# A two-layer perceiver block on one core: who sends the shift row, where the exponents stand and how the column maxima are taken in the second layer's context attention

## The reference, cut to what matters

```python
q = query @ Wq.T + bq
k = key @ Wk.T + bk
v = value @ Wv.T + bv
scores = jnp.einsum('bhtd,bhsd->bhts', q, k) * scale
attn = jax.nn.softmax(scores, axis=-1)
ctx = jnp.einsum('bhts,bhsd->bhtd', attn, v)
return ctx.transpose(0, 2, 1, 3).reshape(B, T, D_MODEL) @ Wo.T + bo
```

## Time and profile before

| What | Value |
|---|---|
| median of 3 runs | 3909.35 us (3906.99 to 3917.72) |
| time of the profiled execution | 3923.12 us, of which the span is 3921.2 us |
| PE busy over the span | 3746.8 us (96%) |
| DVE, ACT, POOL busy | 2212.4, 1525.4 and 1012.3 us |
| the stage that is changed | from about 2427 to 3640 us of the span |

### The profile page before, as it was taken

How to read it: one execution, slowest core, us unless ns; L and a number is a source line. 1 busy time by engine, 2 the same in 40 slices (tenths; PEclk the granted TensorE clock), 3 DMA queues, 4 the chain that set the end, 5 groups by cost and what they waited for, 6 DMA issues and landing times. The chain is left out here.

```text
span 3921.2 us, 73601 instructions
## 1 busy us (share of the span) xinstructions
PE 3746.8 (96%) x29918; PEld 2714.0 (69%) x29918; DVE 2212.4 (56%) x4864; ACT 1525.4 (39%) x3725; POOL 1012.3 (26%) x857
## 2 busy tenths in 40 slices
PE   8999999999999999999999999999999999999897
PEld 4777777777777777867756556666666666667785
DVE  4555555555555545535555413676676766766557
ACT  3233222232323323224433222555555555565444
POOL 2020201011010202002221021354554554553222
PEclk9999999999999999999999999999999999999999
DMA  4112222212121212120040574212212212101100
GB/s 151 61 59 65 65 65 65 65 55 72 48 65 44 80 42 85 54 71 23 24 134 28 169 263 127 63 20 66 65 24 66 63 26 64 52 20 31 37 2 23
DMA packets 159837, 254.81 MB, mean 65 GB/s; under 512 B 28112, under 2 KB 66640, under 8 KB 157712
## 3 DMA queue, kind: packets, MB, share of 16 engines
q1 hardware_dynamic: 121872, 188.15, 15.2%
q0 software_dynamic: 13104, 47.98, 3.7%
q10 hardware_dynamic: 24528, 13.96, 1.7%
HBM read 216.97 MB, written 33.10 MB: 64 GB/s over the span
## 5 line engine op out<-in xcount | busy, mean ns | idle before, releaser
L581 PE MATMUL swishmax_attended<-swishmax_weights_t,swishmax_context 128*128 128x128 f32 x4096 | 520.1, 275 | 3.4 <-DVE swishmax_values_t L505 3.4
L1561 POOL TENSOR_TENSOR context_partial<-context_partial,context_weights_t 128x512 f32<-128x512 f32 x300 | 382.4, 1275 | 466.4 <-ACT context_weights_t L1589 449.9
L435 ACT ACTIVATE swishmax_xes<-swishmax_score,swishmax_neg_max 128x512 f32<-128x512 f32 x256 | 177.1, 694 | 806.9 <-DVE swishmax_neg_max L470 806.9
L581 PEld LDWEIGHTS swishmax_attended<-swishmax_weights_t,swishmax_context 128*128 128x128 f32 x4096 | 487.9, 192 | 3.8 <-issue 3.8
L1770 PE MATMUL context_bank<-ahead_stream,ahead_staged 128*128 128x512 f32 x1024 | 485.3, 617 | 3.1 <-PEq L1138 1.7
L595 PE MATMUL swishmax_bank<-ahead_stream,ahead_w 128*128 128x512 f32 x1024 | 464.2, 596 | 7.4 <-DMA ahead_stream<-in_context_t_dram 7.4
L581 PE MATMUL swishmax_attended<-swishmax_weights_t,swishmax_sides 128*128 128x128 f32 x3072 | 384.9, 275 | 0.0
L581 PEld LDWEIGHTS swishmax_attended<-swishmax_weights_t,swishmax_sides 128*128 128x128 f32 x3072 | 363.6, 192 | 0.0
L1770 PEld LDWEIGHTS context_bank<-ahead_stream,ahead_staged 128*128 128x128 f32 x1024 | 189.0, 195 | 213.4 <-issue 199.0
L1779 PEld LDWEIGHTS context_bank<-ahead_w,ahead_stream 128*128 128x128 f32 x2304 | 276.9, 192 | 80.6 <-issue 55.3
L1670 DVE TENSOR_TENSOR context_weights_t<-context_weights_t,context_spread 128x512 f32<-128x512 f32 x512 | 314.7, 679 | 30.1 <-ACT context_spread L1585 25.9
(11 more groups left out here) (379 smaller groups left out, 5787.3 us busy)
## 6 DMA issues: line engine op xcount, KB each, us to landing
ahead_stream<-in_context_t_dram SPq DMA_DIRECT2D x78, 1024.0 KB, 6.1
swishmax_context<-in_context_dram POOLq DMA_DIRECT2D x32, 1024.0 KB, 5.7
swishmax_down<-_L_xattn_value_down_dram SPq DMA_DIRECT2D x64, 256.0 KB, 4.3
swishmax_up<-in_L_xattn_value_up_dram SPq DMA_DIRECT2D x32, 512.0 KB, 5.9
ahead_values<-ahead_staged SPq DMA_DIRECT2D x14, 1024.0 KB, 8.8
context_values<-ahead_values SPq DMA_DIRECT2D x56, 256.0 KB, 3.2
experts_w<-in_L_ffn_W_dram SPq DMA_DIRECT2D x16, 512.0 KB, 12.4
context_shift<-context_minima ACTq DMA_DIRECT2D x32, 256.0 KB, 4.8
```

The lines of the kernel that those rows point to most:

```text
L435: nc.scalar.activation(xes[:, n % XES, r, :], score[r][:], ACT.Exp, bias=neg_max[:, e, r, c:c + 1]).then_inc(exped, 1)
L581: last = nc.tensor.matmul(product(i)[:, m, :], side(left, c, k, m), weights_t[:, n % 2, right, k, :], start=c == 0 and k == 0 and m == 0 a ...
L1561: link(nc.gpsimd.tensor_tensor(acc, acc, w_t[:, :, k, :], ALU.add))
```

## The change

Six things are edited, all in `softmax_context`.

* The two DMAs of the shift row leave ACT's list. SP sends both, in a new function `send_minima`, after its other loads of each step with c = 3.
* The exponents of heads 2 and 3 of a chunk move one step later on ACT, behind the copies and behind `spread`. Heads 0 and 1 stay at the end of their step.
* `weights_t` has 7 slots in place of 8.
* The maxima are one strided reduction over the 4 tiles of a score bank for each head and chunk, written to its own place in a larger `highest`. `fold` is one strided reduction over the 4 chunks of `highest`. Before, there were 4 or 8 two-input maxima of 256 columns for each chunk.
* On DVE, `heads` stands ahead of the maxima, the shifts always behind them, and `minima` after the first two of four shifts.
* The value bias is no longer added in `heads`. Once, in step 1, PE multiplies it by the output weights (tile `bias`) and DVE adds the product to `bias_o`.

```diff
@@ softmax_context
-    KEYS, VALUES, SLOTS = 5, 12, 8
-    HALF = CH // 2
+    KEYS, VALUES, SLOTS = 5, 12, 7
...
-        highest, folded_max = s.sb("highest", [P, HG, HALF]), s.sb("folded_max", [P, HG, P])
+        highest, folded_max = s.sb("highest", [P, HG, NCH, P]), s.sb("folded_max", [P, HG, P])
...
@@ act_step
-            exps = [("exp", *divmod(n - NCH - 1, NCH), r) for r in range(HG)] * (0 <= n - NCH - 1 < NU * NCH)
-            minima = [(what, u - 1) for what in ("minima_out", "minima_in")] * (c == 0 and 1 <= u <= NU)
-            out = [("copy", u, c, r) for r in range(HG)] * (u < NU) + minima[:1] + [("spread", u - 1)] * (c == 1 and 1 <= u <= NU)
-            values = value_tiles(n)
-            out += [("key", u + 1, c)] * (u + 1 < NU) + values[:len(values) - 1]
-            return out + exps[:2] + minima[1:] + values[-1:] + exps[2:]
+            def exps(m, some):
+                return [("exp", *divmod(m, NCH), r) for r in some] * (0 <= m < NU * NCH)
+
+            out = [("copy", u, c, r) for r in range(HG)] * (u < NU) + [("spread", u - 1)] * (c == 1 and 1 <= u <= NU) + exps(n - LAG, range(2, HG))
+            return out + [("key", u + 1, c)] * (u + 1 < NU) + value_tiles(n) + exps(n - NCH - 1, range(2))
...
@@ dve_step
-            maxima = [("max", u, c)] * (u < NU) + [("fold", u)] * (c == NCH - 1 and u < NU)
+            out = [("heads", u - 2)] * (c == 2 and u >= 2) + [("max", u, c)] * (u < NU) + [("fold", u)] * (c == NCH - 1 and u < NU)
             shifts = [("shift", *divmod(n - NCH - 1, NCH), r) for r in range(HG)] * (0 <= n - NCH - 1 < NU * NCH)
-            heads = [("heads", u - 2)] * (c == 2 and u >= 2)
-            out = maxima + shifts if c == NCH - 1 else shifts + heads + maxima if c == 0 or c == 2 else maxima + shifts
-            out += [("minima", u)] * (c == NCH - 1 and u < NU)
+            out += shifts[:2] + [("minima", u)] * (c == NCH - 1 and u < NU) + shifts[2:] + [("bias", 0)] * (n == 1)
...
@@ block.sync
+                def send_minima(u):
+                    sp.wait_ge(minima_set, u + 1)
+                    sp.dma_start(minima_dram[u].rearrange("r q -> q r"), row_min[:], allow_slow_non_contiguous=True).then_inc(minima_landed, 16)
+                    sp.wait_ge(minima_landed, 16 * (u + 1))
+                    if u:
+                        sp.wait_ge(shift_spread, u)
+                    sp.dma_start(shift[:].rearrange("p r q -> p (r q)"),
+                                 broadcast(minima_dram[u].rearrange("r q -> (r q)"))).then_inc(shift_landed, 16)
...
                     if 1 <= b < B and c < NCH:
                         load_context(b, c)
+                    if n % NCH == NCH - 1 and n > 0:
+                        send_minima(n // NCH)
...
@@ block.vector
                         for r in range(HG):
                             dve.wait_ge(copied, n * HG + r + 1)
-                            if c == 0:
-                                scores_t = weights_t[:, n % SLOTS, r].rearrange("p k q -> p (k q)")
-                                nc.vector.tensor_tensor(highest[:, r], scores_t[:, 0:HALF], score[r][:, HALF:], ALU.max).then_inc(maxed, 1)
-                            else:
-                                last = nc.vector.tensor_tensor(highest[:, r], highest[:, r], score[r][:, 0:HALF], ALU.max)
-                        if c:
-                            link(last)
-                            for r in range(HG):
-                                nc.vector.tensor_tensor(highest[:, r], highest[:, r], score[r][:, HALF:], ALU.max).then_inc(maxed, 1)
+                            nc.vector.tensor_reduce(highest[:, r, c, :], score[r][:].rearrange("p (k q) -> p q k", q=P), AX.X, ALU.max).then_inc(maxed, 1)
                     elif what == "fold":
                         dve.wait_ge(maxed, (u + 1) * NCH * HG)
-                        nc.vector.tensor_tensor(folded_max[:], highest[:, :, 0:P], highest[:, :, P:], ALU.max).then_inc(folded, 1)
+                        nc.vector.tensor_reduce(folded_max[:], highest[:].rearrange("p r c q -> p r q c"), AX.X, ALU.max).then_inc(folded, 1)
...
                         link(nc.vector.reciprocal(inverse[:], attended[:, 1]))
-                        link(nc.vector.tensor_tensor(quotient[:], attended[:, 0], inverse[:], ALU.mult))
-                        nc.vector.tensor_scalar(heads_t[:, b % 2, g, :], quotient[:], bias[:, 2, g:g + 1], None, ALU.add).then_inc(heads_out, 1)
+                        nc.vector.tensor_tensor(heads_t[:, b % 2, g, :], attended[:, 0], inverse[:], ALU.mult).then_inc(heads_out, 1)
```

More of the change, by code:

```diff
@@ L1398, in softmax_context @@
         partial = s.sb("partial", [P, 2, HG, P])
-        inverse, quotient = s.sb("inverse", [P, P]), s.sb("quotient", [P, P])
+        inverse = s.sb("inverse", [P, P])
         queries_t = s.sb("queries_t", [P, 2, NG, P])
@@ L1626, in _ @@
                 first(nc.vector.memset(ones[:], 1.0))
+                for g in range(NG):
+                    last = nc.vector.tensor_scalar(heads_t[:, 1, g, :], ones[:], bias[:, 2, g:g + 1], None, ALU.mult)
+                first(last)
                 first(nc.vector.tensor_scalar(bias_q[:], bias[:, 0, :], SCALE, None, ALU.mult))
@@ L1699, in _ @@
                                                                   op0=ALU.mult, op1=ALU.add)
+                        elif what == "bias":
+                            last = nc.vector.tensor_tensor(bias_o[:], bias_o[:], ring.bank(t)[:], ALU.add)
                         elif what == "output":
@@ L1795, in _ @@
                                                         start=c == 0, stop=c == DC - 1)
+                    elif what == "bias":
+                        pe.wait_ge(w_loaded["o"], 16)
+                        for g in range(NG):
+                            last = nc.tensor.matmul(bank_t[:], heads_t[:, 1, g, :], w["o"][:, g, :], start=g == 0, stop=g == NG - 1)
                     elif what == "output":
```

13 lines of the change are left out of this document (1 added, 12 removed).

## The result

The changed kernel takes 4030.65 us (median of 4, 4022.36 to 4036.04), the kernel before 3908.8 in the same session. The ratio is 1.0305 (95% interval 1.0281 to 1.0329): slower by 122 us, where 56 us were forecast. The profiled execution took 4036.04 us with a span of 4034.2. That is 113 us more than before.

A forecast was written before the change was run, and what follows sets the result against it. Bound: a loop through ACT's wait for the shift row's first DMA, 34 to 36 us a unit. After: 30 x 36.4 = 1092, + 35 + 27 + 21 + 30 = 1205 against 1148.4; execution 3980, median 3965 us, range 3858 to 4030.

The forecast's parts named there:

- S: Start of `spread` on ACT, from which the loop was counted: row issued at S + 22.8, next S at S + 36.4.
- 8.8 to 10.6: Microseconds from issue to landing of the shift row's first DMA in the kernel before; 8.8 taken for the changed loop.
- most of its 8.8 us is not data movement: Shift row's first DMA: engines idle between 2720 and 2724 while it had not landed; part may come from where issued.
- The fold: DVE's reduction of 2048 elements, on the loop before the row's issue: 2.3 us against 1.30 shown before.
- the 1205: Forecast microseconds for the 31 unit intervals, against 1148.4 before: +57 us.
- the strided reads are slow: Rival: reduction elements take twice as long, 2.1 us more for four maxima and for the fold; 4095 us, chance 0.13.
- The clock: Key tile after PE's stall runs partly at the lower clock: 1.2 us for 29 units, 35 us; bounds 0 and 1.7.
- about 34.1 a unit: Seven-slot loop, copy waiting for POOL's chunk, 8.7 us a step; decides only if the 36.4 us DMA loop is shorter.
- the row lands sooner: Rival: row lands sooner from SP, under 7.0 us; at 5 us 64 us less, about 3845 to 3860; chance 0.14.
- The queue behind the context load: In 7 units SP sends 1 MB of context ahead of the row: 0 to 4.5 us, 3 taken, 21 us.
- The query tile: PE's `query` tile between `sums` and the last score in 7 units: 3.84 us each, 27 us.
- The first interval: First unit interval, without attend and sums yet: nearly PE's 26 us with a short stall, 30 us.

The follow-up runs named there:

- before_row16: Kernel before with the shift row stored query by query in 16-byte pieces, spread reading it with a 16-byte step; 3792.33 us, ratio 0.9664.
- exps_late_only: Kernel before with only the exponents of heads 2 and 3 moved a step later, behind spread; 4029.82 us, ratio 1.0306.
- exps_together: Changed kernel with all four exponents of a chunk back at the end of their step; 3866.71 us, ratio 0.9888.
- fold_contiguous: Changed kernel with the chunk index of the maxima innermost, so the fold reads its 2048 elements in order; 3977.68 us, ratio 1.0171.
- late_row16: Changed kernel, exponents still late, with the shift row stored query by query in 16-byte pieces; 3996.43 us, ratio 1.0141.
- together_row16: Changed kernel with all four exponents together, the fold reading in order and the shift row in 16-byte pieces; 3805.08 us, ratio 0.9734.
- fold_step8: Changed kernel with maxima kept in groups of two queries, so the fold steps by 8 bytes; ratio 1.0172.
- fold_step16: Changed kernel with maxima kept in groups of four queries, so the fold steps by 16 bytes; ratio 1.0284.

## Why the prediction was half right

Of the 122 us, 56 were forecast. Of the other 66, 39 are in the unit loop, 18 outside it, and 9 come from which execution was profiled. The step that failed in the loop is the stretch from S to the row's issue: its walk was right, and two of its terms were too small, the fold above all. The step that failed outside is that nothing was reckoned there.

**What bounded the kernel: right.** `before_row16` shows it. The landing of "8.8 to 10.6" was near, with a mean of 9.94 over all units. The reading that "most of its 8.8 us is not data movement", since the DMA engines' share was 0.00, misled: in pieces of 16 bytes the same row took 1.4 us from SP. So the time comes with the small pieces, though hardly any of it shows in that share; where it goes, no run shows.

**Who waits after the change: right.** The moved exponents make `attend`, POOL and `sums` late, and PE stands 3.2 us before `sums`, as forecast. From S (2803.38) POOL starts at S + 1.8 (forecast 1.9) and `sums` at S + 7.2 (7.3). The row goes out at S + 25.5 there, and at S + 25.9 in the mean of the 24 plain units. Forecast were 22.8 and 1.2 for the clock, 24.0. Fold and clock, next, make the difference. `exps_late_only` and `exps_together` show the cause from both sides.

**The fold: mis-sized, the largest miss.** "2.3" for the fold was extrapolated from reads in order, and 2.29 is what it takes in order. It took 3.73. Over 31 units that is 44 us, and `fold_contiguous` gave back 53. With it a plain unit is 37.8 us beside the 37.6 forecast, so there the walk holds. That its profiled execution, 3985 us, is near the 3980 that the sum gave is partly luck: its loop is 12 us shorter than the 1205, and its time outside the loop longer. The rival "the strided reads are slow" was half of the answer: it held for SBUF at 1.63 times, not twice, and not for PSUM, where the maxima step by 512 bytes and take 0.681 us, no more than `row_min` in order, 0.68. The forecast set it aside as a whole, and its range left it out.

**The clock: right in kind, too small.** 1.2 us a unit was forecast, with bounds 0 and 1.7. The 29 key tiles behind `sums` took 5.45 us on average in place of 3.70, so 1.75, above the upper bound. That is 16 us more than forecast.

**The second DMA sets S: right, with the wrong wait.** I had ACT waiting "4 to 6 us a unit" for the row at `spread`. It waited 1.3 us per unit on average, because its copies had stood before that for POOL's sums. Still the DMA loop sets the plain unit: 25.9 from S to the issue, 8.65 to the second issue (forecast 8.8), 4.53 to its landing (4.8) and 0.02 to the next S are the 39.1 measured. What the forecast mispriced is the loop behind it. The seven slots were priced at "about 34.1 a unit" (their own terms give 33.4), to matter only if the DMA loop is shorter. That was a loop of four equal steps; the real one passes through the fold and the slow key tile and takes 37.5 in `late_row16`, 1.6 less than the loop through both DMAs. So the changed kernel has two loops of nearly one length, and shortening either alone gives little: 7 us of landing bought at most 64 us. The same mispricing is in the rival "the row lands sooner": at 5 us it had the kernel 64 us faster than before. `late_row16` takes 1.7 us on average, and is 1.4% slower.

**The queue behind the context load: not here.** I added 3 us to seven units. In five of the seven that have such a load just ahead, the second issue followed 7.1 to 7.8 us after the first, in the two others 8.2 and 9.0; elsewhere it was 7.8 to 10.1. So nothing was later. In `together_row16`, where the row itself needs 1.4 us, the same seven units show 3.6 to 4.9, so there the row does come 2.2 to 3.5 us later behind the load. This fits the ring order that the Trainium skill states (DMA: Bandwidth & Descriptors, Queues, rings and completion order), but engines that are merely shared could do it too, and no run separates the two. With 4-byte pieces it is hidden, for a reason that no run shows.

**The query tile: near by luck.** Six units are 44.5 to 44.7 us, forecast 44.4, which had 3 us for the load that did not come. Against a plain unit they are 5.5 longer, not 3.84: 3.4 from S to the issue, and 2.0 because `spread` there starts 1.5 to 2.5 us after the landing. The seventh, in the second interval, is 41.0.

**The first interval: wrong.** 30 forecast, 37.7 measured. The row's two DMAs, 8.4 and 4.8 us, stand in it as in the others.

The ledger of the intervals: 24 plain ones at 39.1 in place of 37.6 are 36 us, the six with a query 1, the seventh, counted among the 24, -7, the first 8. That is 38 of the 39 us between 1205 and 1244. **Outside the loop** I had nothing, and 18 us are there: the first key tile starts 10.1 us later (2408.78), ahead of any changed code; from it to the first issue it is 5.2 us longer, of which the bias tile is 3.7 and was meant to be paid back; and 2.3 at the end. The first 10 stay open: in the other runs the first key tile started anywhere from 2397 to 2410 us without a pattern in the edits, so it may be the chance of one execution. Last, the profiled execution before lay 14 us above its median, the one after 5 above, which makes the remaining 9.

## What to carry to other kernels

Moving work one step later on an engine that has idle time is free only if nothing downstream was using the distance. Here two exponents behind one copy tied three engines to a DMA, and that cost 3.0 to 4.2% in the five pairs of kernels that differ by it alone (differences of the ratios), also where the row was quick and no DMA was waited for. SP as the sender gained 1.2 to 1.6%, DVE's order 1.2% with the exponents together; the new maxima and the seven slots showed no gain. Price every loop that a change touches by walking it through a trace row by row, also the ones that seem slack: two loops of equal length hide each other's gains. And before reordering around a slow small transfer, look at its pieces; one changed layout was worth more than all the reordering.

## What the runs showed of the hardware

* A DVE reduction over 2048 fp32 elements in SBUF takes 2.29 us in order or with a step of 8 bytes, 3.81 with 16 and 3.73 with 512. ACT's copy of 512 elements goes from 0.60 to 1.14 us with a step of 16. From PSUM, a reduction stepping by 512 bytes costs nothing extra (0.68), nor does writing its results 16 bytes apart (0.684).
* Storing a 2 KB row from 128 partitions in pieces of 4 bytes and waiting for it took 8.6 to 10.2 us in the mean of a run. In pieces of 16 bytes it took 1.4 us in most units from SP, and 3.66 on average from ACT, whose list has other work in between. Between the two sizes, the stage's count of packets under 512 bytes falls by two thirds:

```profile
DMA packets 46417, 59.18 MB, mean 46 GB/s; under 512 B 18886, under 2 KB 18886, under 8 KB 46289
```

  in `fold_contiguous`, and in `late_row16`:

```profile
DMA packets 32909, 56.53 MB, mean 44 GB/s; under 512 B 6496, under 2 KB 6496, under 8 KB 32782
```

* The 4-byte landing also differed between two chips. From issue to issue it took 8.97 us in `fold_contiguous` and 9.72 in `fold_step8`, which has an equally short fold but ran where the kernel before was 29 us slower. `fold_step16`, on that second chip, took 9.38 where the changed kernel, with as long a fold, took 8.64. 32 times 0.74 is 24, so this may be most of the 29; that it is was not shown.
